# Audio tower on one core: queries scaled by their inverse root mean square before the transposes, two score banks instead of three

## What is computed

```python
q = x @ wq.T;  k, v = split(x @ wkv.T)           # 16 query heads, 1 key/value head, 64 wide, 128 tokens
q = rmsnorm(rope(q), q_norm_w)                   # x * rsqrt(mean(x*x) + eps) * w
k = rmsnorm(rope(k), k_norm_w)
scores = where(mask, (q @ k.T) / sqrt(64), -1e30)   # causal
out = softmax(scores) @ v
return out @ wo.T
```

## Time and profile before

| | us |
|---|---|
| median of 3 runs | 2186.41 (2185.26 to 2187.06) |
| the profiled execution | 2186.65 |
| its span, first to last instruction | 2184.9 |
| PE busy over the span | 1961.2 (90%) |
| DVE busy | 1599.8 (73%) |
| ACT busy | 1455.9 (67%) |
| POOL busy | 780.3 (36%) |
| mean granted PE clock, share of full | 0.970 |

### The profile page before, as it was taken

How to read it: one execution, slowest core, us unless ns; L and a number is a source line. 1 busy time by engine, 2 the same in 40 slices (tenths; PEclk the granted TensorE clock), 3 DMA queues, 4 the chain that set the end, 5 groups by cost and what they waited for, 6 DMA issues and landing times. The chain is left out here.

```text
span 2184.9 us, 33132 instructions
## 1 busy us (share of the span) xinstructions
PE 1961.2 (90%) x9572; PEld 1374.9 (63%) x9637; DVE 1599.8 (73%) x3563; ACT 1455.9 (67%) x3736; POOL 780.3 (36%) x1416
## 2 busy tenths in 40 slices
PE   1899999999999699999589999999999999968998
PEld 0677777777777578777355555555555555535554
DVE  3578887888877556665588888888888888845554
ACT  0467776776766434444388888888888888844554
POOL 0122222222222003222566655655665565532100
PEclk9999999999999799999599999999999999978999
DMA  4111111111110000000000000000000000000000
GB/s 135 44 34 40 40 34 44 35 39 42 32 44 22 1 1 1 1 1 1 1 1 1 1 1 1 1 1 1 1 1 1 1 1 1 1 1 6 10 11 15
DMA packets 28095, 35.61 MB, mean 16 GB/s; under 512 B 13740, under 2 KB 14380, under 8 KB 27660
## 3 DMA queue, kind: packets, MB, share of 16 engines
q1 hardware_dynamic: 27916, 33.49, 5.4%
HBM read 12.09 MB, written 2.10 MB: 6 GB/s over the span
## 5 line engine op out<-in xcount | busy, mean ns | idle before, releaser
L1389 ACT ACTIVATE apb<-ps,anb,arq 128x128 f32<-128x128 f32 x1024 | 454.4, 454 | 79.8 <-DVE anb L1264 77.1
L1497 POOL TENSOR_TENSOR apb<-apb,arc 128x512 f32<-128x512 f32 x256 | 266.1, 1040 | 324.1 <-DVE arc L1272 321.2
L1143 PE MATMUL ps<-akT,aqT 128*128 128x256 f32 x1024 | 266.8, 384 | 5.6 <-issue 2.8
L1258 DVE TENSOR_REDUCE amx<-ps 128x4 f32<-128x512 f32 x256 | 175.5, 686 | 115.1 <-PE ps L1143 114.2
L1143 PEld LDWEIGHTS ps<-akT,aqT 128*128 128x128 f32 x1024 | 199.2, 195 | 21.8
L516 DVE SCALAR_TENSOR_TENSOR h0l<-ps,h0h 128x1024 fp32r<-128x1024 f32 x128 | 156.0, 1219 | 74.2 <-ACT h0h L441 74.2
L1154 PE MATMUL ps<-const,apb 128*128 128x128 f32 x1024 | 159.0, 278 | 54.9 <-POOL apb L1497 52.2
L1389 ACT ACTIVATION_READ_ACCUMULATOR apb<-ps,anb,arq 128x1 f32 x1024 | 204.5, 200 | 0.0
L65 PE MATMUL ps<-h0h,w123h 128*128 128x512 f32 x512 | 204.1, 399 | 0.0
L67 PE MATMUL ps<-h0h,w123l 128*128 128x512 f32 x512 | 203.5, 397 | 0.0
L66 PE MATMUL ps<-h0l,w123h 128*128 128x512 f32 x512 | 203.5, 397 | 0.0
(11 more groups left out here) (300 smaller groups left out, 4903.4 us busy)
## 6 DMA issues: line engine op xcount, KB each, us to landing
x0k<-x0h SPq DMA_DIRECT2D x128, 72.0 KB
x<-in_x SPq DMA_DIRECT2D x32, 192.0 KB, 2.6
x0k<-x0l SPq DMA_DIRECT2D x64, 72.0 KB
x0k<-x0h SPq DMA_DIRECT2D x64, 48.0 KB
out<-fyo SPq DMA_DIRECT2D x16, 128.0 KB, 2.0
x0k<-x0l SPq DMA_DIRECT2D x32, 48.0 KB
w<-in_w SPq DMA_DIRECT2D x1, 1024.0 KB, 6.9
mw<-in_mw SPq DMA_DIRECT2D x1, 1024.0 KB, 8.7
```

The source lines that it names most:

```text
L1143: last = pe.matmul(bank[:, p * 2 * T:(p + 1) * 2 * T], qT[:, i % 2, 2 * k + p, :], kT[:, i // 4 % 2, i % 4, :, :].rearrange("p a s -> p (a ...
L1258: ve.tensor_reduce(mx[:, k, :], ps[:, SB[n % 3], :].rearrange("p (h s) -> p h s", h=4), AX_X, ALU.max, negate=True).then_inc(S["mx"], 1)
L1389: last = ac.activation(pb[:, i % 2, head, :], ps[:, SB[n % 3], h * T:(h + 1) * T], ACT.Exp, bias=nb[:, k, h:h + 1], scale=rq[:, i % 2, hea ...
L1497: po.tensor_tensor(p, p, rc[:, i % 2, 4 * k:4 * k + 4].unsqueeze(2).to_broadcast([T, 4, T]), ALU.mult).then_inc(S["pn"], 1)
```

## The change

All of it is in `attention_phase`.

- `rms_q` works by half: Ln and Exp of 8 columns, 128 times each, instead of 16 columns, 64 times. A new POOL step `scale_q` multiplies a half of `aqr` in place by `arq`, broadcast over 64 columns; `q_t` waits for it (semaphore `qm`) in place of `sq` and `qr`.
- The product L1264 and its tile `anb` go. The exponentials take `amx` as bias and have no scale operand.
- `q_t` writes into bank 2 (QT), alone there, and waits for the copy of the half before; the scores have banks 0 and 1 and wait for the exponentials n-2.
- The tables move: projection four slots earlier, `q_t` two slots earlier, `normal_x` two slots earlier, `p_t` three slots after its scores (two before), `p_v` and `w_o` and `turn` two slots later, `k_t` one later. `avs` has three buffers (two before). The first quad starts 22 slots ahead of the first scores (18 before).
- On DVE `recip(u - 1)` stands ahead of `p_copy`; residual and statistics stand one slot nearer to `turn`.

The diff, without most of its context:

```diff
-    SB, QB, TB, OB, XB = (0, 1, 2), (3, 4), 5, 6, 7
+    SB, QB, QT, TB, OB, XB = (0, 1), (3, 4), 2, 5, 6, 7
     def first(q):
-        return 16 * (q - 1) if q else -14
+        return 16 * (q - 1)
     def by_slot(count, slot):
...
-    at_xn = {first(q) - 4 + n: (q, n) for q in range(QUADS) for n in range(4)}
+    at_xn = {first(q) - 6 + n: (q, n) for q in range(QUADS) for n in range(4)}
...
-    at_kt = by_slot(QUADS, lambda q: first(q) + 12)
-    at_q = by_slot(HALVES, lambda m: 4 * (m // 2) - 5 + 2 * (m % 2))
-    at_qt = by_slot(HALVES, lambda m: 4 * (m // 2) - 3 + 2 * (m % 2))
-    at_rms = by_slot(B, lambda i: 4 * i - 1)
-    at_pt = by_slot(PARTS, lambda n: n + 2)
-    at_pv = by_slot(HALVES, lambda m: 4 * (m // 2) + 4 + 2 * (m % 2))
-    at_wo = {16 * (q + 1) + 4 + c: (q, c) for q in range(QUADS) for c in range(4)}
-    at_tr = by_slot(QUADS, lambda q: 16 * (q + 1) + 9)
-    SLOTS = range(first(0) - 4, max(at_tr) + 4)
+    at_kt = by_slot(QUADS, lambda q: first(q) + 13)
+    at_q = by_slot(HALVES, lambda m: 4 * (m // 2) - 9 + 2 * (m % 2))
+    at_rms = by_slot(HALVES, lambda m: 4 * (m // 2) - 7 + 2 * (m % 2))
+    at_qm = by_slot(HALVES, lambda m: 4 * (m // 2) - 6 + 2 * (m % 2))
+    at_qt = by_slot(HALVES, lambda m: 4 * (m // 2) - 5 + 2 * (m % 2))
+    at_pt = by_slot(PARTS, lambda n: n + 3)
+    at_pv = by_slot(HALVES, lambda m: 4 * (m // 2) + 6 + 2 * (m % 2))
+    at_wo = {16 * (q + 1) + 6 + c: (q, c) for q in range(QUADS) for c in range(4)}
+    at_tr = by_slot(QUADS, lambda q: 16 * (q + 1) + 11)
+    SLOTS = range(first(0) - 6, max(at_tr) + 4)
...
-        vs = sb("avs", [T, 2, 4, DH])
+        vs = sb("avs", [T, 3, 4, DH])
...
-        rq = sb("arq", [T, 2, NH])
+        rq = sb("arq", [T, NH])
...
-        nb = sb("anb", [T, 4, 4])
...
-                 "q", "rope", "sq", "qr", "ssq", "lrq", "rq", "qt", "qT", "s", "mx", "nb", "ex", "rc", "pn", "pt", "pT",
+                 "q", "rope", "sq", "qr", "ssq", "lrq", "rq", "qm", "qt", "qT", "s", "mx", "ex", "rc", "pn", "pt", "pT",
...
                 def project(m):
...
-                        pe.wait_ge(S["qT"], m - 1)
+                        pe.wait_ge(S["sq"], m - 1)
...
                 def q_t(m):
...
-                    pe.wait_ge(S["sq"], m + 1)
-                    pe.wait_ge(S["qr"], m + 1)
+                    if m >= 1:
+                        pe.wait_ge(S["qT"], m)
+                    pe.wait_ge(S["qm"], m + 1)
...
-                        last = pe.transpose(ps[:, QB[h], p * T:(p + 1) * T], qr[:, h, p * 2 * DH:(p + 1) * 2 * DH],
+                        last = pe.transpose(ps[:, QT, p * T:(p + 1) * T], qr[:, h, p * 2 * DH:(p + 1) * 2 * DH],
...
                 def scores(n):
...
-                    if n >= 3:
-                        pe.wait_ge(S["ex"], n - 2)
+                    if n >= 2:
+                        pe.wait_ge(S["ex"], n - 1)
...
-                    bank = ps[:, SB[n % 3], :]
+                    bank = ps[:, SB[n % 2], :]
...
-                        last = pe.matmul(ps[64 * odd:64 * odd + 64, OB, :], vs[:, i // 4 % 2, i % 4, :],
+                        last = pe.matmul(ps[64 * odd:64 * odd + 64, OB, :], vs[:, i // 4 % 3, i % 4, :],
...
-                    if q >= 2:
-                        ve.wait_ge(S["pv"], 8 * (q - 1))
-                    ve.tensor_copy(vs[:, q % 2, :, :], kv[:, :, DH:2 * DH]).then_inc(S["vs"], 1)
+                    if q >= 3:
+                        ve.wait_ge(S["pv"], 8 * (q - 2))
+                    ve.tensor_copy(vs[:, q % 3, :, :], kv[:, :, DH:2 * DH]).then_inc(S["vs"], 1)
...
                 def sum_q(m):
...
-                    if i >= 1 and h == 0:
-                        ve.wait_ge(S["lrq"], i)
+                    if i >= 1:
+                        ve.wait_ge(S["lrq"], m - 1)
...
                 def maximum(n):
-                    i, k = n // 4, n % 4
...
                     if n >= 4:
-                        ve.wait_ge(S["nb"], n - 3)
-                    ve.tensor_reduce(mx[:, k, :], ps[:, SB[n % 3], :].rearrange("p (h s) -> p h s", h=4), AX_X, ALU.max,
+                        ve.wait_ge(S["ex"], n - 3)
+                    ve.tensor_reduce(mx[:, n % 4, :], ps[:, SB[n % 2], :].rearrange("p (h s) -> p h s", h=4), AX_X, ALU.max,
...
-                    ve.wait_ge(S["mx"], n + 1)
-                    ve.wait_ge(S["rq"], i + 1)
-                    if n >= 4:
-                        ve.wait_ge(S["ex"], n - 3)
-                    ve.tensor_tensor(nb[:, k, :], mx[:, k, :], rq[:, i % 2, 4 * k:4 * k + 4], ALU.mult
-                                     ).then_inc(S["nb"], 1)
...
                 for u in SLOTS:
...
+                    if 0 <= u - 1 < PARTS:
+                        recip(u - 1)
...
-                    if 0 <= u - 1 < PARTS:
-                        recip(u - 1)
...
-                    if u - 1 in at_tr:
-                        residual(at_tr[u - 1])
-                    if u - 3 in at_tr:
-                        statistics(at_tr[u - 3])
+                    if u in at_tr:
+                        residual(at_tr[u])
+                    if u - 2 in at_tr:
+                        statistics(at_tr[u - 2])
...
-                def rms_q(i):
-                    ac.wait_ge(S["ssq"], 2 * i + 2)
-                    ac.activation(lrq[:], ssq[:], ACT.Ln, bias=epsc[:, 1:2], scale=1.0 / DH).then_inc(S["lrq"], 1)
-                    ac.wait_ge(S["lrq"], i + 1)
-                    if i >= 2:
-                        ac.wait_ge(S["nb"], 4 * (i - 1))
-                    ac.activation(rq[:, i % 2, :], lrq[:], ACT.Exp, scale=-0.5).then_inc(S["rq"], 1)
+                def rms_q(m):
+                    i, h = m // 2, m % 2
+                    heads = slice(8 * h, 8 * h + 8)
+                    ac.wait_ge(S["ssq"], m + 1)
+                    ac.activation(lrq[:, heads], ssq[:, heads], ACT.Ln, bias=epsc[:, 1:2], scale=1.0 / DH
+                                  ).then_inc(S["lrq"], 1)
+                    ac.wait_ge(S["lrq"], m + 1)
+                    if i >= 1:
+                        ac.wait_ge(S["qm"], m - 1)
+                    ac.activation(rq[:, heads], lrq[:, heads], ACT.Exp, scale=-0.5).then_inc(S["rq"], 1)
                 def keep_q(m):
...
-                    ac.activation(qT[:, i % 2, 4 * h:4 * h + 4, :], ps[:, QB[h], :].rearrange("p (h t) -> p h t", h=4),
+                    ac.activation(qT[:, i % 2, 4 * h:4 * h + 4, :], ps[:, QT, :].rearrange("p (h t) -> p h t", h=4),
...
                 def exps(n):
...
-                    ac.wait_ge(S["nb"], n + 1)
+                    ac.wait_ge(S["mx"], n + 1)
...
-                        last = ac.activation(pb[:, i % 2, head, :], ps[:, SB[n % 3], h * T:(h + 1) * T], ACT.Exp,
-                                             bias=nb[:, k, h:h + 1], scale=rq[:, i % 2, head:head + 1],
-                                             accum_out=sm[:, i % 2, head:head + 1])
+                        last = ac.activation(pb[:, i % 2, head, :], ps[:, SB[n % 2], h * T:(h + 1) * T], ACT.Exp,
+                                             bias=mx[:, k, h:h + 1], accum_out=sm[:, i % 2, head:head + 1])
...
                 def keep_o(m):
...
+                def scale_q(m):
+                    h = m % 2
+                    po.wait_ge(S["rq"], m + 1)
+                    po.wait_ge(S["qr"], m + 1)
+                    q = qr[:, h, :].rearrange("p (h d) -> p h d", h=8)
+                    po.tensor_tensor(q, q, rq[:, 8 * h:8 * h + 8].unsqueeze(2).to_broadcast([T, 8, DH]), ALU.mult
+                                     ).then_inc(S["qm"], 1)
+
...
+                    if u in at_qm:
+                        scale_q(at_qm[u])
...
```

## The result

| | before | after |
|---|---|---|
| median, us | 2185.84 (4 runs) | 2107.94 (4 runs, 2105.99 to 2110.98) |
| ratio | | 0.9648, 95% interval 0.9630 to 0.9666 |
| profiled execution, us | 2186.65 | 2106.76 |

The kernel became 78 us faster, twice what was forecast (38). The direction was right; the size was not.

A forecast was written before the change was run, and what follows sets the result against it. PE was taken to set the pace: its 46.55 us floor plus 0.5 clock, 0.3 gaps and 2.85 scaling wait made 50.2 against 53.05 a period. 2186.65 - 45.4 + 7 for the start = 2148 us, range 2105 to 2182.

The forecast's parts named there:

- PE's floor: PE's own work in attention, summed from slots without waits: 46.55 us per period of 16 slots, unchanged by the change.
- both waits of the earlier trace: PE's probability transposes waiting for POOL's normalisation, 47.6 us, and x transposes waiting for x, 21.2 us; both would go.
- the scale operand's 86 ns: On ACT, each of 1024 exponentials without its scale operand would be 86 ns shorter than 454 ns; bounds 0 and 86.
- two banks at no cost: Scores waiting for exponentials two slots back on two banks would have 1.3 us to spare; costed at nothing.
- the start: First scores stand behind the third half's `q_t`, so the first maximum comes near 1090: 7 us lost, bounds 3 and 10.
- Rival (b): `q_t` does not wait, because POOL's sum stands earlier: period 47.35 us, time 2103 us; chance 0.14.
- The wait for the scaling: PE's `q_t` would wait for POOL's `scale_q`, worst in slots 5 (1.7 us) and 13 (0.9): 2.85 us a period.
- Clock and small gaps carried over: Added to PE's period after the change: 0.5 us for the granted clock, taken as now, and 0.3 for small gaps.
- The period before: Attention's pace before, from its 256 maxima: 53.05 us per 16 slots, 15.94 periods; the gain was counted from it.
- The end of attention: The tail was said to have the same chain, one lag longer in name only; no time was booked.
- The likeliest case: The forecast itself: period 50.2 us, time 2148 us, own range 2130 to 2167; chance 0.57.
- The product is slack: Removing L1264 between maximum and exponentials takes 0.16 us of chain per slot, booked as slack on DVE, not as time.

The follow-up runs named there:

- b1: The kernel before with only the pieces of x two slots earlier (`at_xn`): 2156.72 us, ratio 0.9878.
- b3: The kernel before with the table shifts and three `avs` buffers, but projection and `q_t` in old places, product, scale operand and three score banks kept: 2097.12 us, ratio 0.9601.

## Why the prediction was wrong, step by step

The steps that held: PE's floor, 46.55 forecast and 46.49 measured; both waits of the earlier trace rows gone; the scale operand's 86 ns; ACT not the limit; two banks at no cost; the start, 7 us forecast and 7.3 measured; that q_t would wait, in slots 5 and 13 and a little in 15, and nowhere else that counts. Rival (b), "q_t does not wait", is not what happened either: q_t waits. That the time lies within 5 us of its 2103 is chance.

The term that was mis-sized is the period: 50.2 forecast, 48.49 measured, against 53.05 used for before. Four parts, with 15.94 periods each:

1. *The wait for the scaling*: 2.85 forecast, 1.98 measured (1.35 in slot 5, 0.52 in 13, 0.11 in 15). 14 us. For slot 5 the forecast says 1.7, though its own terms (0.5 late, 0.7 for k's sum, 0.3 for DVE) make 1.5. The timeline above gives 1.3: the four POOL steps take 3.94 us from 1193.19 to 1197.13 where the terms make 4.09, since their records overlap by some 0.05 each, and the chain starts 4.04 us after its slot's scores, not 4.15.
2. *Clock and small gaps carried over*: 0.8 forecast, none measured. 13 us. A remainder that I couldn't explain before I kept as if it were a constant. It belonged to the waits. The clock's 0.5 belonged to the wait for x, as b1 shows: the clock is 1.00 with that wait gone and nothing else changed. The 0.3 of small gaps fit gaps recorded too short; that they went with the waits is read from the floor and the table, and no run splits them off.
3. *The period before*: I took 53.05, the mean over all 255 slots, and set it against a floor for a full period. The first and last slots lack w_o, k and x work; a full period before is 53.54. 8 us.
4. *The end of attention*: 3.3 us, booked at nothing. About 2 us more were in the phases before attention, which the change doesn't touch, so these are the luck of one execution.

Together 14 + 13 + 8 + 3 + 2 = 40, and 1 more for the floor (46.49, not 46.55): the 41 us between 2148 and the profiled 2106.76.

The likeliest case's own range ended at 2130 and failed with the forecast. The whole range, down to 2105, holds the measured time by 3 us, and by luck: its lower end came from rival (b), whose 2103 still contained the 0.8 of point 2 and lacked the 0.5 of point 3. Put right, "no wait" is 2082, and the measured time would have lain well inside.

Two steps had the wrong reason though they didn't decide the time. "The product is slack" was false for the changed kernel: put back, it costs 29 us. The forecast took 0.16 us for it from the median of the earlier trace rows, where the mean is 0.39. What it cost in the kernel before, no run shows alone; b3 keeps it and is still faster than the change. And the order of reciprocal and copy was listed in the front and priced nowhere; alone it is worth 29 us in the kernel before, and costs 0.3% beside the shifts.

## What to carry to other kernels

Add up the limiting engine's own work for one full period from slots without a wait; what stands above it is what a change of schedule can win, all of it, the unexplained remainder included. When two parts of a change remove the same wait, try each alone: here the shifts of places alone (2097) beat the whole change (2108), and the change with one POOL step moved ahead of a step that has time (2085) beats both. A small step on an engine that is not the limit still costs time when it stands ahead of the work for which the limiting engine waits. Ask for the mean of such a step, not only for the median.

## What the runs showed of the hardware

A [128,1] scale operand adds 87 ns to a 128x128 exponential with bias and accumulated sum (367 to 454 ns). A 128x4 DVE product of two SBUF inputs takes 161 ns at the least and up to 862 ns when a POOL instruction is running as it starts; the long ones (185 of 256) end 16 to 23 ns after that instruction. A 128x4 reduction in the same place takes 157 to 158 ns throughout. Back-to-back POOL products of 1.04 us started 0.99 us apart. Gaps of PE are recorded short: at a granted clock of 1.00, a wait recorded at 1.15 us made its slot 1.35 us longer. The recorded 21.2 us of waits for x were worth 26.5 us, and there the clock is in it: four stretches of some 3 us at 0.50 in the kernel before, none without the waits. The last output projection, 16 matmuls, took 3.65 us at a clock of 1.00 and 5.72 us in a stretch with a mean of 0.68.
